# First group: the table product ahead of the third mixing step, weight tiles made by one or two, the first two in halves

## What is computed

```python
def _L0_cond_ref(x, weights, condition):          # a 64x64 mixing matrix for each batch
    W = weights[condition]
    return jnp.einsum('bct,bcd->bdt', x, W)

def _L0_ffn_ref(x, W_base, b_base, enc0, enc1, coefs0, coefs1, mask0, mask1):
    base = jnp.einsum('bsd,od->bso', x, W_base) + b_base
    e0 = jnp.einsum('bsd,rd->bsr', x, enc0)       # rank 32
    e1 = jnp.einsum('bsd,rd->bsr', x, enc1)       # rank 8
    w0 = coefs0 * mask0.astype(coefs0.dtype)
    w1 = coefs1 * mask1.astype(coefs1.dtype)
    decoded = jnp.einsum('bsr,eor->ebso', e0, w0) + jnp.einsum('bsr,eor->ebso', e1, w1)
    transformed = real_fourier_orthogonal_multiply(decoded)   # irfft over the 1024 outputs
    return base + transformed.sum(axis=0) * 0.5

x = x + _L0_ffn_ref(_L0_cond_ref(x, L0_cond_weights, itok_B_0_15), ...)
x = x + _L1_ffn_ref(_L1_cond_ref(x, ..., itok_B_2_6, 0), L1_ffn_weight, L1_ffn_bias)
```

## Time and profile before

| what | value |
|---|---|
| median of 3 runs | 1947.08 us (1946.88 to 1948.09) |
| the profiled execution's own time | 1948.11 us |
| its span, first to last instruction | 1946.4 us |
| busy: PE, DVE, ACT, POOL | 98%, 77%, 39%, 28% |
| mean granted TensorE clock | 0.996 |
| HBM over the span | 112 GB/s |

### The profile page before, as it was taken

One profiled execution on the slowest core, in us unless ns is written; L12 is line 12 of the kernel. 1 busy time (PEld: TensorE's weight loads), 2 busy tenths in 40 slices (PEclk: granted clock), 3 DMA queues, 4 the chain that ended last, 5 costly groups with the idle time before them and its releaser, 6 DMA issues.

```text
span 1946.4 us, 31433 instructions
## 1 busy us (share of the span) xinstructions
PE 1917.0 (98%) x9072; PEld 1606.9 (83%) x9072; DVE 1493.7 (77%) x2482; ACT 762.8 (39%) x1450; POOL 541.1 (28%) x933
## 2 busy tenths in 40 slices
PE   6999999999999999999999999999999999999998
PEld 5888888888988888888898888888889888888886
DVE  6977777778778777777777877777877777777785
ACT  3453333334344333333344433333325443333431
POOL 6342222213415212221523322212071322222100
PEclk8999999999999999999999999999999999999999
DMA  9675445543476454443446655555335655555411
GB/s 246 148 146 109 104 99 115 120 94 82 126 150 126 104 116 101 103 100 79 119 121 139 125 110 120 107 107 110 81 88 132 124 121 120 109 118 111 103 32 44
DMA packets 320566, 219.43 MB, mean 113 GB/s; under 512 B 177129, under 2 KB 311145, under 8 KB 320481
## 3 DMA queue, kind: packets, MB, share of 16 engines
q1 hardware_dynamic: 282976, 190.00, 43.6%
q0 software_dynamic: 36352, 24.19, 6.9%
q10 hardware_dynamic: 1152, 4.19, 0.6%
HBM read 205.40 MB, written 12.58 MB: 112 GB/s over the span
## 4 chain that ended last, share of the span: by engine, by line
PE 92%; DVE 4%; ACT 2%; issue 2%; DMA 0%; POOLq 0%; DVEq 0%; ACTq 0%; POOL 0%
PE ps L1351 26%; PE ps L1353 25%; PE ps L1352 25%; PE ps L1559 6%; PE ps L1485 2%; PE ps L1405 2%; PE ps L1406 2%; DVE ps L854 2%; PE ps L1377 1%; DVE split L840 1%; PE ps L1424 1%; PE ps L1375 1%; ACT split L591 0%; ACT hidden L591 0%; PE ps L1596 0%
## 5 line engine op out<-in xcount | busy, mean ns | idle before, releaser
L1351 PE MATMUL ps<-x,split 128*128 128x512 f32 x1376 | 538.2, 391 | 1.2 <-DVE split L840 1.2
L1353 PE MATMUL ps<-x,split 128*128 128x512 f32 x1376 | 536.8, 390 | 0.0
L1352 PE MATMUL ps<-x,split 128*128 128x512 f32 x1376 | 535.9, 389 | 0.0
L591 ACT ACTIVATE split<-ps 128x512 fp32r<-128x512 f32 x344 | 202.9, 599 | 451.1 <-DVE ps L854 439.1
L490 POOL DMA_DIRECT2D nat_ad<-L_cond_A_down x224 | 136.9, 618 | 733.6 <-DVE ps L854 724.2
L1353 PEld LDWEIGHTS ps<-x,split 128*128 128x128 f32 x1376 | 258.4, 188 | 55.7
L1352 PEld LDWEIGHTS ps<-x,split 128*128 128x128 f32 x1376 | 258.6, 188 | 54.6
L1351 PEld LDWEIGHTS ps<-x,split 128*128 128x128 f32 x1376 | 259.1, 188 | 49.8 <-DVE split L840 2.5
L1351 PE MATMUL ps<-hidden 128*128 128x512 f32 x672 | 262.2, 390 | 0.0
L1352 PE MATMUL ps<-hidden 128*128 128x512 f32 x672 | 261.8, 390 | 0.0
L1353 PE MATMUL ps<-hidden 128*128 128x512 f32 x672 | 261.6, 389 | 0.0
(11 more groups left out here) (127 smaller groups left out, 2762.1 us busy)
## 6 DMA issues: line engine op xcount, KB each, us to landing
nat<-L_cond_W_gate SPq DMA_DIRECT2D x336, 128.0 KB
nat<-L_cond_W_up SPq DMA_DIRECT2D x336, 128.0 KB
nat_down<-L_cond_W_down SPq DMA_DIRECT2D x112, 384.0 KB, 6.5
nat_a<-L_ffn_weight SPq DMA_DIRECT2D x128, 128.0 KB, 2.8
nat<-effective_weight SPq DMA_DIRECT2D x24, 512.0 KB
nat<-x SPq DMA_DIRECT2D x16, 512.0 KB
nat_b<-L_cond_B_gate POOLq DMA_DIRECT2D x224, 24.0 KB, 2.2
nat_b<-L_cond_B_up POOLq DMA_DIRECT2D x224, 24.0 KB, 2.1
```

Source lines behind the costliest of these rows:

```text
L591: act.activation(dst, src, func).then_inc(piece_hi, 1)
L1351: pe.matmul(dst, a[0], b[0], start=first, stop=False)
L1352: pe.matmul(dst, a[0], b[1], start=False, stop=False)
L1353: return pe.matmul(dst, a[1], b[0], start=False, stop=last)
```

## The change

- SP's order at the start: x tile 0, coefficients, the table, x tiles 1 and 2, W_base tile 0, enc, x tile 3, W_base tiles 1 to 3, then as before.
- On PE the table product stands ahead of mixing step 2 instead of step 6. ACT and DVE get an order of their own for the mixing of group 0 (`mixing_first`). `adapter_sum` stands right behind the first x tile's low word.
- ACT makes the first copy of enc and reads out half of the table product; DVE makes low_s in two pieces of columns (`LOW_COLUMNS`: those of tiles 0 to 2, then the rest).
- Five products make the weight tiles, `MADE` = (0), (1, 2), (3, 4), (5, 6), (7), in place of four pairs. (0) stands ahead of mixing step 5 and goes into banks 6 and 7; (1, 2) stands between the halves of x1 tile 0, (3, 4) between those of tile 1, (5, 6) ahead of tile 3, (7) ahead of tile 5. Each from the third on waits for the adds of the product before.
- Weight tiles 0 and 1 are added, copied and made low in halves of their columns (`half_added`, `half_hi`, `half_lo`), and `first_layer` takes its first half behind the first of them.
- In DVE's loop each iteration u = 0 to 4 adds tile 3 + u, the same that it makes low further on in the iteration; ACT stores it there too. PE waits ahead of x1 tile 6 for seven adds instead of eight.

The diff, without declarations, the bodies of the new word-making helpers and what the lines above say in full:

```diff
-WEIGHT_BANKS = 2
+MADE = ((0,), (1, 2), (3, 4), (5, 6), (7,))
+MADE_BANKS = (6, 2, 2, 2, 4)
+MADE_OF = {u: (v, n) for v, tiles in enumerate(MADE) for n, u in enumerate(tiles)}
+LOW_COLUMNS = (slice(0, 96), slice(96, 256))
...
-            for p in range(3):
-                load_x(0, p)
+            load_x(0, 0)
             for i in range(2):
                 sp.dma_start(coef[i], coefs[i].rearrange("e (p c) r -> p e (c r)", c=KC)).then_inc(coef_in, 16)
                 sp.dma_start(coef_mask[i], masks[i].rearrange("e (p c) r -> p e (c r)", c=KC)).then_inc(coef_in, 16)
-            load_x(0, 3)
+            table_rows = fourier.rearrange("(p c) n -> p c n", c=KC)
+            for i in range(4):
+                sp.dma_start(table[:, 2 * i:2 * i + 2], table_rows[:, 2 * i:2 * i + 2]).then_inc(table_in[i], 16)
+            for p in range(1, 3):
+                load_x(0, p)
+            load_base(0)
             for n in range(3):
                 sp.dma_start(enc[R0 * n:R0 * n + R0, :], enc0).then_inc(enc_in, 16)
                 sp.dma_start(enc[3 * R0 + R1 * n:3 * R0 + R1 * n + R1, :], enc1).then_inc(enc_in, 16)
-            table_rows = fourier.rearrange("(p c) n -> p c n", c=KC)
-            for i in range(4):
-                sp.dma_start(table[:, 2 * i:2 * i + 2], table_rows[:, 2 * i:2 * i + 2]).then_inc(table_in[i], 16)
-            for u in range(BASE_SLOTS):
+            load_x(0, 3)
+            for u in range(1, BASE_SLOTS):
...
+            def made_halves(u):
+                slot_read(0, 0, SPLIT_W + u)
+                hi = split[:, (SPLIT_W + u) % SPLIT_SLOTS, 0, :]
+                act.wait_ge(half_added, u + 1)
+                copy(hi[:, 0:512], base_t[:, u, 0:512]).then_inc(half_hi, 1)
+                act.wait_ge(w_added, u + 1)
+                copy(hi[:, 512:], base_t[:, u, 512:]).then_inc(plain_hi, 1)
+            def mixing_first():
+                plain_unit(0, 0, NAT_X, SPLIT_X)
+                cond(0, 0)
+                for e in range(2):
+                    mixing(0, e)
+                for p in (1, 2):
+                    plain_unit(0, p, NAT_X + p, SPLIT_X + p)
+                    cond(0, p)
+                    if p == 1:
+                        act.wait_ge(enc_in, 96)
+                        copy(enc_s.rearrange("r k (q d) -> r q k d", q=4),
+                             enc.rearrange("r (q k d) -> r q k d", q=4, k=KC)).then_inc(enc_step, 1)
+                act.wait_ge(enc_step, 2)
+                act.wait_ge(g_psum, 1)
+                copy(enc[:, 0:512], ps[0:STACK, 6, :]).then_inc(g_moved, 1)
+                mixing(0, 2)
+                plain_unit(0, 3, NAT_X + 3, SPLIT_X + 3)
+                mixing(0, 3)
+                cond(0, 3)
+                mixing(0, 4)
+                made_halves(0)
+                for e in range(5, 8):
+                    mixing(0, e)
+                store_weight(0)
+                made_halves(1)
+                store_weight(1)
+                made_unit(2)
+                store_weight(2)
...
-                    if making and u in (0, 1, 3, 4):
-                        store_weight(u + 4 - u // 3)
+                    if making and u < 5:
+                        store_weight(3 + u)
...
             def add_weight(u):
+                v, n = MADE_OF[u]
                 dve.wait_ge(base_turned, u + 1)
-                dve.wait_ge(w_psum, u // 2 + 1)
+                dve.wait_ge(w_psum, v + 1)
                 tile = base_t[:, u].rearrange("p (k o) -> p k o", k=KC)
-                made = ps[:, WEIGHT_BANKS:WEIGHT_BANKS + 4, :].rearrange("p a (k n o) -> p (a k) n o", k=2, n=2)
-                dve.tensor_tensor(tile, made[:, :, u % 2, :], tile, ALU.add).then_inc(w_added, 1)
-            def stacked(dst, src, column, done):
-                low = own_sb[0:STACK, GB + column:GB + column + 1]
-                dve.tensor_copy(dst, src).then_inc(g_read, 1)
-                dve.wait_ge(g_read, done)
-                parts = [(dst[:, q], src[:, q]) for q in range(4)] if len(dst.shape) == 4 else [(dst, src)]
-                for to, full in parts:
-                    last = dve.scalar_tensor_tensor(out=to, in0=to.bitcast(F32), scalar=low, in1=full, op0=ALU.mult,
-                                                    op1=ALU.add)
-                last.then_inc(g_read, 1)
-            def low_rank_rows(e):
-                if e == 1:
-                    adapter_sum()
-                if e == 3:
-                    dve.wait_ge(enc_in, 96)
-                    stacked(enc_s.rearrange("r k (q d) -> r q k d", q=4),
-                            enc.rearrange("r (q k d) -> r q k d", q=4, k=KC), 0, 1)
-                if e != 6:
-                    return
+                tiles = len(MADE[v])
+                made = ps[:, MADE_BANKS[v]:MADE_BANKS[v] + 2 * tiles, :]\
+                    .rearrange("p a (k n o) -> p (a k) n o", k=4 // tiles, n=tiles)[:, :, n, :]
+                if u < 2:
+                    dve.tensor_tensor(tile[:, 0:4], made[:, 0:4], tile[:, 0:4], ALU.add).then_inc(half_added, 1)
+                    dve.tensor_tensor(tile[:, 4:], made[:, 4:], tile[:, 4:], ALU.add).then_inc(w_added, 1)
+                else:
+                    dve.tensor_tensor(tile, made, tile, ALU.add).then_inc(w_added, 1)
...
+            def mixing_first():
+                plain_unit(0, 0, NAT_X, SPLIT_X)
+                adapter_sum()
+                cond(0, 0)
+                for e in range(2):
+                    mixing(0, e)
+                plain_unit(0, 1, NAT_X + 1, SPLIT_X + 1)
+                cond(0, 1)
+                enc_words()
+                plain_unit(0, 2, NAT_X + 2, SPLIT_X + 2)
+                cond(0, 2)
+                low_rank_out()
+                low_rank_words(0)
+                mixing(0, 2)
+                plain_unit(0, 3, NAT_X + 3, SPLIT_X + 3)
+                mixing(0, 3)
+                cond(0, 3)
                 turn_base(0)
-                near, far = low_rank[:, 0:H // 2], low_rank[:, H // 2:H]
-                dve.wait_ge(g_psum, 1)
-                dve.tensor_copy(near, ps[0:STACK, 6, :]).then_inc(g_read, 1)
-                dve.wait_ge(g_read, 3)
-                dve.tensor_tensor(far, near, ps[0:STACK, 7, :], ALU.subtract).then_inc(g_read, 1)
-                dve.wait_ge(g_read, 4)
-                dve.tensor_tensor(near, ps[0:STACK, 7, :], near, ALU.add).then_inc(g_read, 1)
-                dve.wait_ge(g_read, 5)
-                stacked(low_s, low_rank, 1, 6)
-            def effective_weight():
+                mixing(0, 4)
+                add_weight(0)
+                made_low_half(0, 0)
+                mixing(0, 5)
+                made_low_half(0, 1)
+                mixing(0, 6)
                 turn_base(1)
-                add_weight(0)
+                mixing(0, 7)
+                low_rank_words(1)
+                add_weight(1)
                 turn_base(2)
-                made_unit(0)
-                add_weight(1)
+                for half in range(2):
+                    made_low_half(1, half)
+                add_weight(2)
                 turn_base(3)
-                made_unit(1)
-                add_weight(2)
-                turn_base(4)
                 made_unit(2)
-                add_weight(3)
-                for u in range(5, KC):
+                for u in range(4, KC):
                     turn_base(u)
 
             def first_layer_all(g, making):
                 for u in range(KC):
                     x1_total(g, u)
-                    if making and u in (0, 1, 3, 4):
-                        add_weight(u + 4 - u // 3)
+                    if making and u < 5:
+                        add_weight(3 + u)
...
+                by_halves = g == 0 and u < 2
+                if not by_halves:
+                    pe.wait_ge(plain_lo, 12 * g + 4 + u + 1)
                 if half == 0:
                     pe.wait_ge(mixed_lo, 8 * g + 4)
                 if g == 0 and u == 6:
-                    pe.wait_ge(w_added, KC)
+                    pe.wait_ge(w_added, KC - 1)
...
+                    if by_halves and half == 0 and k == 0:
+                        pe.wait_ge(half_lo, u + 1)
+                    if by_halves and half == 0 and k == 4:
+                        pe.wait_ge(plain_lo, 4 + u + 1)
...
-                    if e == 6 and making:
+                    if e == 2 and making:
                         low_rank_product()
+                    if e == 5 and making:
+                        make_weights(0)
...
-            def weight_pair(v):
+            def make_weights(v):
+                tiles = MADE[v]
                 if v == 0:
-                    pe.wait_ge(g_read, 7)
+                    pe.wait_ge(low_step, 3)
+                elif v == 1:
                     pe.wait_ge(mixed_lo, 8)
                     pe.wait_ge(xt_copied, 8)
                 else:
-                    pe.wait_ge(w_added, 2 * v)
+                    pe.wait_ge(low_step, 6)
```

(52 more changed lines are left out.)

17 lines of the change are left out of this document (5 added, 12 removed).

## The result

The changed kernel takes 1952.11 us (median of 10 runs, 1950.1 to 1958.58), the kernel before, run beside it, 1947.89 us (10 runs, 1946.62 to 1948.56): ratio 1.0026, 95% interval 1.0018 to 1.0035. It is 4.2 us slower, just beyond the 0.2% (3.9 us) that the prediction counts as no change, on the side to which it gave 0.44; the time lies in its range. The rows from here to the experiments are those of the slowest execution.

What follows compares the result with a forecast made beforehand. PE, busy 98% of the span, was taken as the bound, so gains come only from its stalls. Ranks at 95.1 instead of 91.53 us add 3.5 to 1948.11: 1951.6, as a median 1950.6 us, range 1946.5 to 1953.8.

Steps and rivals of the forecast that it cites:

- The main mechanism: At make_weights(3), PE idles some 7 us for DVE's add of tile 4, then works at the lower clock.
- signs of being wrong: No PE wait at the fourth product, first x1 total before 51, ACT awaiting enc beyond 22 us, or ranks moving without the total.
- last turn, wait for base 7: DVE's last turn waits for base 7, landed at 54.4 us and turned at 55.6, where DVE's loop begins.
- iteration 0 of DVE's loop: DVE's first loop iteration takes 6.1 us instead of 4.78, with the add in it and a wait for ACT.
- enc late: Rival: ACT waits for enc ahead of hi x2; landing at 24.5 us gives +6.5, 1953.6 us; chance 0.13.
- The base of the median: Profiled execution 1948.11 us, median 1947.08, so 1.0 us taken off 1951.6 to give 1950.6.
- The clock: Behind PE's pause at make_weights(3) the lower clock costs 2.2 us, between 1.5 and 2.8.
- The fifth product: Tile 7's own weight product on PE, eight matmuls 128 columns wide, takes 0.85 us, bounds 0.5 and 0.96.
- adapter_sum ahead of the first cond: On DVE at the start: costs 0, but coefficients landing after 8.8 us delay the start one for one.
- The constants: Their loads on SyncE's queue are issued no later than before, with base 1 to 3; costed at nothing.
- lead kept: Rival: PE does not wait at make_weights(3), so ranks come 4.7 us earlier, 1942.4 us; chance 0.06.
- The table is not there: Rival: PE waits for the table with mixing steps 2 to 7 behind; landing at 20 us +2.5, 1953.1; chance 0.05.

Runs made afterwards that it cites:

- add_ahead: Changed kernel with the adds of weight tiles 3 to 7 one iteration earlier, as in the kernel before; 1945.33 us, ratio 0.9991.
- after_again: The changed kernel once more, unedited, for a second profile; 1952.32 us, ratio 1.0023; its profiled execution took 1953.14 us.
- enc_ahead: Changed kernel with enc's six loads moved between the table and x1; 1951.69 us, +3.7 from the kernel before.
- busy_pe: Changed kernel with 24 unused matmuls put on PE ahead of make_weights(3) to keep it at work through the pause; 1950.61 us.
- old_order: Changed kernel with SyncE's first loads in the order of the kernel before; 1951.51 us, ratio 1.0016.
- add_turn7: Changed kernel with the adds of tiles 3 to 7 one iteration earlier and turn_base(7) in DVE's iteration 2; 1944.22 us, ratio 0.9985.
- coef_first: Changed kernel, adds of tiles 3 to 7 an iteration earlier, turn_base(7) in iteration 2, loads x0, coefficients, x1 to x3, enc, table, base; 1943.05 us.
- add_turn7_old: Changed kernel, adds of tiles 3 to 7 an iteration earlier, turn_base(7) in iteration 2, first loads in the old order; 1944.2 us, ratio 0.9984.
- product_early: Kernel before with the table product's new place alone, behind mixing step 1; adds, weight pairs and loads as before; 1948.54 us, ratio 1.0006.

## Why the prediction came out as it did

The main mechanism was right and so was its place: PE stands still 6.2 us at make_weights(3) for DVE's add, the clock falls, and add_ahead takes 7 us off by undoing the one edit that the prediction named. But one of its own signs of being wrong came true beside it: ACT waits for enc beyond 22 us. That the number came so close has a share of luck: the prediction passes the lateness of enc on us for us, and part of it is lost on the way. By its steps, with the ordinary execution first and the slowest in brackets:

| step | predicted | after_again (after) |
|---|---|---|
| first mixing step | 12.2, up to 1 later | 12.64 (14.47) |
| table product | 17.5 to 24.9 | 17.90 to 25.3 (19.02 to 26.0) |
| ACT has enc | 21 to 22 | 24.16 (29.49) |
| DVE's read-out | 25.5 | 28.18 (33.51) |
| PE's tile 2 | 51 | 53.42 (58.83) |
| end of turn 3 | 47.3 | 49.4 (54.8) |
| last turn, wait for base 7 | 54.4, 2.5 | 56.20, 2.14 (60.97, 0.59) |
| first x1 total | 55.6 | 57.37 (62.13) |
| iteration 0 of DVE's loop | 6.1 | 5.89 (5.90) |
| PE free, make_weights(3) | 56.5, 63.7 | 59.05, 65.29 (64.47, 70.06) |
| from there to ranks | 31.4 | 31.31 (32.04) |
| ranks | 95.1 | 96.60 (102.10) |

The predicted wait for base 7 is 54.4 less 51.9: the row of turns would end at 53.1 without it, so the last turn, of 1.16, would begin at 51.9. PE's lead at tile 2 is 3.9 us (57.32 to 53.42), not 6; in the slowest execution there is none, and in add_ahead tile 2 is at 51.18, the predicted place.

- **The step that was off is enc.** I costed its transfer at 209 GB/s behind base 0, landing at 21 to 22 us; it was 24.2 and 29.5. In the slowest execution the last of its loads was issued at 13.05 us and landed 16.4 us later:

```profile
13.05 16.42 DMA enc<-L_ffn_enc
```

The windows there carried 250, 206 and 204 GB/s (15 to 20, 20 to 25, 25 to 30 us), so the rate was right. So was the volume: what SyncE's queue holds up to the end of enc is some 5.4 MB, and that much had been moved by 20.5 us in after_again and 21 us in the slowest execution, against 20.1 in the sum. What failed is the order: the sum has enc complete before anything behind it in the queue. The queues (SyncE's q1, GpSimd's q0: packets, MB, share) up to the moment at which enc is there, 0 to 24.1 us of after_again (first two lines) and 0 to 29.4 us of the slowest:

```profile
q1 hardware_dynamic: 4008, 6.06, 91.8%
q0 software_dynamic: 256, 0.13, 2.0%
q1 hardware_dynamic: 4539, 6.56, 83.0%
q0 software_dynamic: 953, 0.70, 13.5%
```

So 0.7 and 1.2 MB of loads that stand behind enc (x3, base 1 to 3) had been moved before its last bytes. GpSimd's queue had moved no more than the 0.13 MB that the sum counts in after_again, and 0.6 MB more in the slowest. Why enc's last bytes stay behind is open; no run takes the other loads away. This is the rival "enc late", which had 0.13, and it came true beside the forecast; the median, 1952.1, lies between the two (1950.6 and 1953.6). Its price was too high: the lateness counts in full at DVE's read-out (2.7 us in after_again), but 1.8 us of it are left at the first x1 total and 1.5 at ranks. Between the medians the result is +4.2 us where I had +3.5. By the Trainium skill, "DMA: Bandwidth & Descriptors", Specifications, the ceiling of 435 GB/s would have had enc there by an estimated 17 us (3.06 MB behind 10 us; the prediction says 16). The trace has 196 to 250 GB/s from 15 us on, while enc is on its way, and stays far below that ceiling.
- **The base of the median.** I took 1.0 us off for the profiled execution's place among three runs. Ten runs give 1947.89, 0.2 below it. With that the same sum says 1951.4. The 0.7 us from there to 1952.1 fit the step above (enc_ahead takes off 0.6), but a difference so small is within the spread of the runs.
- **The clock** was priced at 2.2 us; busy_pe measures 1.7 to 1.9, and 2.6 against the slowest execution.
- **The fifth product.** From 84.86 us to the next matmul at 85.70 it takes 0.84 us, inside my bounds of 0.5 and 0.96. The Trainium skill, "TensorE: Matmul & The Clock Gate", LDWEIGHTS, gave an estimated 0.86: the trace agrees.
- **adapter_sum ahead of the first cond.** Costed at nothing while the coefficients land by 8.8 us. They did (adapter sum from 8.13 us in after_again), by the new load order; old_order takes the cover away and the price is there: DVE waits 3.3 us for the coefficients, and the start is at 14.3 us. In the slowest execution the start is late for another reason, the cond weights (13.69 us on ACT against 11.86), and 1.3 us beyond the 0 to 1 that I allowed.
- **The constants**, at nothing because "issued no later than before", were issued later: from 26.06 us (after_again) and 30.66 (slowest) against 22.93. No engine waits for them.
- **The rival "lead kept"** named ranks at 86.8 us and 1942.4 us as what PE had truly won, and asked for a loop of DVE that begins at 48 us. add_ahead comes within 1.6 us of these ranks (88.35) with a loop that begins at 55.08: with the adds an iteration ahead, the early loop is not needed. By medians it keeps 2.7 of the 4.7 us; add_turn7 and coef_first, which hold more edits than the change, reach 3.6 and 4.7. **"The table is not there"** fell for the changed kernel, in which PE never waits for it. coef_first shows its price where the table stands last and the start is early: 2.1 us.

## What to carry to other kernels

When a pipelined helper step moves into the iteration that uses it, price both ends: the engine that now waits for it inside its loop (here DVE, 1.1 and 1.2 us in its first two iterations), and the queue of the engine whose next step needs it (here PE, 6 us and a clock drop), even where each step stays equally long. A gain won early can be lost where the engine behind it (DVE's loop) does not start earlier by as much; find what holds that start, here a load whose buffer comes free only four turns before the turn that needs it. Volume over rate gives the time of a group of loads, not of one load in it. When a first load is moved, follow each consumer's queue: here the coefficients mattered for a cond that never reads them.

## What was not expected of the hardware

- The kernel before repeats within 2 us (1946.62 to 1948.56 in ten runs; 1946.93 to 1950.23 in the widest of the other sets, of 33); the changed one spreads over 8.5 us (1950.1 to 1958.58) and 4.9 us in eleven more. Two executions show what differs: enc's landing at 24.2 and 29.5 us, and the cond weights at 11.9 and 13.7 us. Loading enc earlier did not narrow the spread (1950.4 to 1954.8, and 1944.6 to 1950.5 with the adds ahead). The spread goes with the load order: 1.7 to 2.9 us in the three experiments with the old one (old_order, add_turn7_old, product_early), 2.3 to 8.5 wherever the coefficients stand right behind x0, in coef_first too (6.0), whose table stands last. Its cause stays open; that DMA traffic meets differently from run to run is only argued.
- How long SyncE's queue is busy issuing the same loads is not fixed: the twelve issues of base 1 to 3 took 16.6 us in the slowest execution, 13.0 in after_again and 7.9 in add_ahead, which has the same loads in the same order; base's first sixteen took 10.2 before and 13.2 in old_order. What stands behind them on the queue is issued later by as much. What holds the issues up was not tested.
